# Block quantisation on the vector engine: magnitude thresholds taken from the scaled value instead of from the square of the input

## The reference, cut to what matters

```
def _mx_quantize(t, eps=1e-30):            # blocks of 32 features
    blocks = t.reshape(rows, K // 32, 32)
    scales = jnp.maximum(jnp.max(jnp.abs(blocks), axis=-1) / 7.5, eps)
    q = _nearest_on_grid(blocks / scales[..., None], _GRID)
    return (q, scales)

xq, xs = _mx_quantize(x2)                  # x2: layer-normed rows, 4096 x 1024 a core
wq, ws = _mx_quantize(w2)                  # w2: 1024 x 1024
out = (xq * xs) @ (wq * ws).T + bias
x = x + 0.5 * out
```

## Time and profile before

| | us |
|---|---|
| time before, median of 2 runs | 27812.44 |
| the 2 runs | 27726.81 and 27898.06 |
| the profiled execution, its own time | 28129.55 |
| span of its slowest core, core 7 | 28127.9 |
| spans of its other cores | 27678.4 to 28053.1 |
| VectorE busy, core 7 | 16990.2 (60%) |
| TensorE busy, core 7 | 7113.5 (25%) |

### The profile page before, as it was taken

One profiled execution on the slowest core, in us unless ns is written; L12 is line 12 of the kernel. 1 busy time (PEld: TensorE's weight loads), 2 busy tenths in 40 slices (PEclk: granted clock), 3 DMA queues, 4 the chain that ended last, 5 costly groups with the idle time before them and its releaser, 6 DMA issues.

```text
span 28127.9 us, 129139 instructions; the slowest of 8 cores (27678.4 to 28127.9 us)
## 1 busy us (share of the span) xinstructions
PE 7113.5 (25%) x32704; PEld 3383.9 (12%) x32704; DVE 16990.2 (60%) x19236; ACT 5399.3 (19%) x12042; POOL 1095.7 (4%) x2039
## 2 busy tenths in 40 slices
PE   1177896000000000032255543200000000004555
PEld 0033342000000000010133311000000000002333
DVE  7510001799999999857422224489999999983222
ACT  0020004222222222210011112522222222221111
POOL 0010000000000000000000021000000000000000
PEclk6587786555555555565677766555555555557788
DMA  0132203211101101140200033421111111125000
GB/s 31 42 85 61 48 30 73 49 17 29 29 17 29 29 17 29 37 132 33 51 23 23 18 95 114 115 43 26 20 29 22 24 29 19 27 67 155 23 23 21
DMA packets 761522, 1253.66 MB, mean 45 GB/s; under 512 B 117072, under 2 KB 447312, under 8 KB 756688
## 3 DMA queue, kind: packets, MB, share of 16 engines
q1 hardware_dynamic: 545056, 791.44, 11.5%
q0 software_dynamic: 178864, 386.83, 5.6%
q10 hardware_dynamic: 36864, 67.13, 0.6%
HBM read 937.13 MB, written 437.31 MB: 49 GB/s over the span
## 4 chain that ended last, share of the span: by engine, by line
DVE 45%; PE 23%; DVEq 12%; issue 4%; ACT 4%; DMA 4%; SPq 3%; another core or an unknown queue 2%; POOL 1%; ACTq 1%; POOLq 0%
DVEq L180 11%; DVE Bs L180 8%; DVE Es L180 8%; PE Bpcv L180 8%; DVE Etr L180 4%; DVE Btr L180 4%; DVE Bball L180 4%; DVE Eball L180 4%; SPq L180 3%; PE DpsS L180 2%; PE Dps L180 2%; PE FpsS L180 2%; PE Fps L180 2%; PE Epmm L180 2%
## 5 line engine op out<-in xcount | busy, mean ns | idle before, releaser
L180 DVE TENSOR_TENSOR_SCAN Bs<-Babb,Bcarry,Bball 128x256 f32<-128x256 f32 x4096 | 2659.3, 729 | 40.3 <-ACTq L180 3.0
L180 DVE TENSOR_TENSOR_SCAN Es<-Eabb,Ecarry,Eball 128x256 f32<-128x256 f32 x4096 | 2659.2, 729 | 40.3 <-ACTq L180 3.0
L180 ACT ACTIVATE Babb<-Bdd,Ba_sb 128x256 f32<-128x256 f32 x4096 | 1662.9, 494 | 5090.2 <-DVEq L180 5090.1
L180 ACT ACTIVATE Eabb<-Edd,Ea_sb 128x256 f32<-128x256 f32 x4096 | 1662.9, 494 | 5074.4 <-DVEq L180 5074.2
L180 PE MATMUL Bpcv<-Bup,Bcw 128*128 128x512 bf16 x8192 | 2122.9, 431 | 291.9 <-DMA Bcw<-m_conv_w 291.9
L180 PE MATMUL Bpm<-Bwout_sb,Bygb 128*128 128x512 bf16 x1024 | 240.0, 400 | 7141.7 <-DVEq L180 7141.7
L180 PE MATMUL Epm<-Ewout_sb,Eygb 128*128 128x512 bf16 x1024 | 241.0, 401 | 7048.3 <-DVEq L180 7048.3
L180 DVE TENSOR_TENSOR Bdstg<-Bsp 128x512 f32<-128x512 f32 x128 | 88.6, 692 | 2870.6 <-ACTq L180 2870.6
L180 DVE TENSOR_TENSOR Babb<-Bs,BdC 128x4096 f32<-128x4096 f32 x256 | 1131.4, 4419 | 240.8 <-DMA BdC<-Bbc_h 240.6
L180 DVE TENSOR_TENSOR Eabb<-Es,EdC 128x4096 f32<-128x4096 f32 x256 | 1131.3, 4419 | 177.0 <-DMA EdC<-Ebc_h 176.8
L180 DVE TENSOR_TENSOR Eball<-Edlu,EdB 128x4096 f32<-128x4096 f32 x256 | 1132.9, 4425 | 20.7 <-issue 1.7
(11 more groups left out here) (364 smaller groups left out, 14577.0 us busy)
## 6 DMA issues: line engine op xcount, KB each, us to landing
Bup<-Bupre_h SPq DMA_DIRECT2D x256, 129.0 KB, 6.1
Eup<-Eupre_h SPq DMA_DIRECT2D x128, 258.0 KB, 8.8
Bres_h<-Brstg POOLq DMA_DIRECT2D x128, 256.0 KB, 13.2
Bcw<-m_conv_w POOLq DMA_DIRECT2D x128, 256.0 KB, 47.9
Bu_h<-Bustg ACTq DMA_DIRECT2D x128, 256.0 KB, 5.6
Bdel_h<-Bdstg SPq DMA_DIRECT2D x128, 256.0 KB, 4.3
Bdd<-Bdel_h SPq DMA_DIRECT2D x256, 128.0 KB, 3.5
Bdu<-Bu_h SPq DMA_DIRECT2D x256, 128.0 KB, 2.8
```

The costliest lines, as they stand in the source:

```text
L180: r = a(*args, **kw)
```

## The change

The square of the input, its two scaled copies and the square of the scale are no longer made. The scaled value `v` is made first; it is squared into `q4`, and the two flags come from comparing that square with the constants 4 and 16. Two drains are added, ahead of the square and behind it. The scratch tiles `xsq`, `q16` and `scq` are gone. Everything behind the two flags is as before.

```diff
     V.reduce_max(t["sc0"][:, :], v3(src), axis=AX, apply_absolute_value=True)
-    V.tensor_tensor(t["xsq"][:, :], src[:, :], src[:, :], ALU.mult)
     V.drain()
     V.tensor_scalar(t["sc"][:, :], t["sc0"][:, :], 1.0 / 7.5, 1e-30,
                     ALU.mult, ALU.max)
-    V.tensor_scalar(t["q4"][:, :], t["xsq"][:, :], 0.25, None, ALU.mult)
-    V.tensor_scalar(t["q16"][:, :], t["xsq"][:, :], 0.0625, None, ALU.mult)
     V.drain()
     V.reciprocal(t["si"][:, :], t["sc"][:, :])
-    V.tensor_tensor(t["scq"][:, :], t["sc"][:, :], t["sc"][:, :], ALU.mult)
     V.drain()
     V.tensor_tensor(v3(t["v"]), v3(src), sc_b(t["si"]), ALU.mult)
-    V.tensor_tensor(v3(t["g2"]), v3(t["q4"]), sc_b(t["scq"]), ALU.is_ge)
-    V.tensor_tensor(v3(t["g4"]), v3(t["q16"]), sc_b(t["scq"]), ALU.is_ge)
+    V.drain()
+    V.tensor_tensor(t["q4"][:, :], t["v"][:, :], t["v"][:, :], ALU.mult)
+    V.drain()
+    V.tensor_scalar(t["g2"][:, :], t["q4"][:, :], 4.0, None, ALU.is_ge)
+    V.tensor_scalar(t["g4"][:, :], t["q4"][:, :], 16.0, None, ALU.is_ge)
     V.drain()
...
-         for k in ["v", "xsq", "q4", "q16", "g2", "g4", "w1", "sn", "tt",
+         for k in ["v", "q4", "g2", "g4", "w1", "sn", "tt",
                    "z", "rr", "gt", "ff"]}
-    for k in ["sc0", "sc", "si", "scq"]:
+    for k in ["sc0", "sc", "si"]:
```

## The result

| | us |
|---|---|
| changed kernel, median of 40 runs | 27791.41 (27532.73 to 28161.73) |
| kernel before, median of 39 runs | 28056.36 (27710.31 to 28326.96) |
| ratio of the changed kernel to the one before | 0.9932, 95% interval 0.9903 to 0.9961 |
| profiled execution of the changed kernel, span of its slowest core, core 5 | 27846.6 |

The account below looks back on a forecast made before the run. VectorE and what it waits for were taken to form one serial chain in stages A and C. Calls (157 us) plus bursts (16) gave 173 us off 27812, so 27640 us, range 27490 to 27800.

Parts of the forecast that it names:

- The serial chain: Stages A and C: VectorE and its waits form one chain, so time off a quantisation call comes off the stage.
- The call: One quantisation call in A or C saves 1.96 us; eighty calls save 157 us.
- The comparison with a constant: Both flags in a quantisation call: the pair of comparisons takes 1.37 us, drain included.
- the row of stage D: Stage D's one-input comparison takes 486 ns on 128 x 512, as does stage E's multiplication, so comparing costs no more.
- The added drain: Two per quantisation call: each missing overlap costs about 0.15 us.
- The rival of free drains: Quantisation calls: the two added drains cost nothing, saving 181 us in all, 27615 us; chance 4%.
- the term of the matmul bursts: 16-matmul bursts in A and C: mean goes from 6.01 to 5.76 us, gaining 64 x 0.25 = 16 us.
- the bursts settle on one pattern: Bursts in A and C hold one length, short (27583 us) or long (27694 us); chance 25%.
- Its short end: All bursts in A and C at 4.89 us, 72 us gained, 27583 us; chance 17%.
- The mean burst before: Stage A, kernel before: 33.30 us a tile less 27.29 outside the burst gives 6.01 us.
- The sum: Whole kernel: 157 us from calls plus 16 from bursts, 173 us, 0.6% less.
- The step on what can be told: Whole kernel: about 2% (556 us) is distinguishable from no change; within 2% got 98%, faster and slower 1% each.

Follow-up runs that it names:

- the reordered pair: Main loop reordered so VectorE quantises the next rows before taking up this tile's matmuls, with the changed quantisation and that of before: stage C 977.0 and 1055.6 us.
- the drains alone: Kernel before with only the two added drains: stage C 1283.1 us, 29.5 more than before.
- the four other values of the table: Kernel before; changed kernel with one or two VectorE operations more a tile, or two fewer a call: stage C 1253.6, 1182.3, 1209.5, 1121.1 us.
- the three that hold a period: Kernel before plus the two drains, changed kernel, changed kernel with one VectorE operation fewer a call: stage C 1283.1, 1157.9 and 1150.6 us.
- the loop with the extra matmuls and the changed quantisation: Changed kernel plus 36 matmuls a tile with unused results, run while VectorE quantises: stage C 1130.7 us.

## Why the prediction was right or wrong

**The serial chain was right.** A and C got shorter by what their tiles got shorter, and the later stages moved with them. No wait for a load or store appeared.

**The call was right to 0.01 us**: 1.96 predicted, 1.97 in the timeline, 1.965 from the reordered pair. The comparison with a constant, the one price that the trace lacked at its shape, takes 1.37 us for a pair with its drain, as taken; the row of stage D was the right neighbour. The added drain was put at 0.15 us, and the drains alone showed 0.17. The rival of free drains took half of what the Trainium skill says ("VectorE: DVE Perf Modes", The DRAIN you can't avoid): that the next operation does not start until the pipe is empty. The same section adds that an operation that is not held starts earlier. The trace agrees with the addition: the square starts 1.14 us after an operation of 1.22 without a drain and 1.30 with one.

**The step of the sum that failed is the term of the matmul bursts.** The prediction took the middle of the shortest and the longest burst, 5.76 us, and 16 us gained for both stages. In the changed kernel the mean burst is 5.33 us (stage C, core 3), and the bursts brought 34 us, twice the term. Taking the middle was the failed choice: it treated the length as drawn from a spread, when it follows from how long after the burst's beginning the clock rises. The rival "the bursts settle on one pattern" is what happened, at a length between the two ends it was priced at. Its short end, 4.89 us, was priced soundly, since a short burst shortens its tile in full: in the kernel before (stage C, core 3) 27.31 us lie behind the burst of 4.89 at 12665.15 and 27.32 behind that of 6.33 at 12631.50. The loop was not drawn to that end.

**The mean burst before was put at 6.01 and measures 5.91** over the 32 bursts of stage A on core 7. The 27.29 us outside the burst were read from one tile; a minority of tiles, behind short and long bursts alike, have up to 27.67, and the mean is 27.39.

**The sum** was 173 us against 191, and a ratio of 0.9938 against 0.9932 measured. It came near because the calls, 157 us of it, were right; the rest was half of what it should have been.

**The step on what can be told failed as well.** The chances were given for 2%, "about what a measurement of this kernel can tell from no change", and almost all went to "within 2%", while the text itself forecast 0.6% less. With 40 runs the interval is 0.3% to either side, and the kernel is clearly faster. A mechanism with every term priced, which came out within a tenth of its size, should have been stated as the forecast of a faster kernel.

**The level** was 151 us too low: 27640 against 27791. That is not the change. The sum was hung on a median of two runs, 27812, and 39 runs put the kernel before at 28056. That the median of the changed kernel fell into the range, by 9 us, is luck of this level and no sign for the mechanism.

## What to carry to other kernels

Before crediting a saving in a loop where VectorE and short TensorE bursts take turns, look whether the bursts of equal work have equal lengths. If they differ, read the granted clock from the beginning of a burst to its end; if it rises within the burst, as here, small edits elsewhere in the tile can be worth nothing or double. Compare such edits by the length of the stage, or with the bursts off the chain, and repeat with one operation more and one fewer before believing a small gain. The cure is to let VectorE do the next tile's work while the burst runs; here it was worth 181 us a stage, about twice the edit itself.

## What the runs showed of the hardware that was not expected

A loop that is paced by VectorE can hold its period against its own work. At 25.4 and at 24.6 us outside the burst the tiles came every 30.74 and 30.73 us, and at 27.7 every 34.09, with all bursts nearly equal; at the four other values of the table, bursts of the same 16 matmuls went from 4.89 to 6.57 us. The pull can be read in the granted clock: the rises keep a spacing of their own (30.7 or 34.1 us in the kernel before and in the three that hold a period), so a burst that begins later runs less of its work at 1.2 GHz and takes less time, 0.494 us for each us, which brings the next tile back. That the moments have a course of their own agrees with the Trainium skill ("TensorE: Matmul & The Clock Gate", Part 1), which calls the window of the activity monitor free-running; the page does not say that a loop can settle on it. Why the loop with the extra matmuls and the changed quantisation keeps the higher level in some tiles and not in others was not tried further.
